# Attention softmax: row sums from ScalarE over query-major scores, one reciprocal and one transpose a unit

## The reference

```python
q = _rotary((_ln(x, qn_w, qn_b) @ q_w + q_b) ...); k = _rotary(...)      # per head
qn, kn = _ln(q, ln_w, ln_b), _ln(k, ln_w, ln_b)
scores = jnp.einsum('bhqd,bhkd->bhqk', qn, kn) / np.sqrt(HD)
attn = jax.nn.softmax(scores, axis=-1)
a = jnp.einsum('bhqk,bhkd->bhqd', attn, v)
x = layernorm(x + a @ out_w + out_b)
```

## Time and profile before

| | us |
|---|---|
| median of 3 runs | 2387.8 (2382.08 to 2388.36) |
| profiled execution | 2387.83 |
| its span | 2385.8 |
| attention phase within it, to the last row of its output sum | about 1277 |
| one pass of the loop (four units), 310.22 to 457.20 | 146.98 |
| busy PE, DVE, ACT, POOL over the span | 82%, 66%, 38%, 40% |

### The profile page before, as it was taken

The page is one execution under the profiler, slowest core; times in us unless marked ns, Lnnn a source line. Parts: engine busy times, 40 slices in busy tenths (PEclk is TensorE's granted clock), DMA queues, the critical chain, the costliest instruction groups (busy, mean ns, idle before and its releaser), DMA issues. The chain is left out here.

```text
span 2385.8 us, 30230 instructions
## 1 busy us (share of the span) xinstructions
PE 1949.7 (82%) x9560; PEld 1408.7 (59%) x9560; DVE 1564.9 (66%) x2942; ACT 913.2 (38%) x1532; POOL 955.1 (40%) x849
## 2 busy tenths in 40 slices
PE   4588887988889889899884999999948887878872
PEld 4455554655555556556533888887836665666651
DVE  4558578586785857757654666767544776777765
ACT  2134343443433444344342222222214555555653
POOL 1657657576565756657520222222101211221121
PEclk9689999999999999999887999999978998999885
DMA  4132132221322213222214121111031121022111
GB/s 130 27 89 54 28 106 48 84 53 44 88 53 79 53 50 81 53 62 54 67 49 149 50 83 58 53 53 53 18 110 36 53 71 54 18 70 71 54 36 53
DMA packets 90746, 148.67 MB, mean 62 GB/s; under 512 B 16560, under 2 KB 19632, under 8 KB 90672
## 3 DMA queue, kind: packets, MB, share of 16 engines
q1 hardware_dynamic: 90672, 147.76, 20.8%
HBM read 63.82 MB, written 33.55 MB: 41 GB/s over the span
## 5 line engine op out<-in xcount | busy, mean ns | idle before, releaser
L464 DVE TENSOR_REDUCE a_neg_max<-a_max 128x1 f32<-128x512 f32 x512 | 340.2, 686 | 255.4 <-PE a_max L720 250.3
L626 ACT ACTIVATE a_probs<-a_exp 128x512 f32<-128x512 f32 x512 | 291.0, 595 | 546.9 <-PE a_exp L735 542.5
L697 PE MATMUL a_t<-a_w_hi,a_zT_hi 128*128 128x384 f32 x512 | 200.1, 391 | 98.9 <-DVE a_v L430 87.7
L720 PE MATMUL a_max<-a_stack 96*128 96x512 f32 x512 | 228.4, 472 | 40.0 <-DVE a_neg_max L464 35.8
L311 POOL TENSOR_TENSOR a_rstd<-a_rstd,a_minus_half 128x16 f32<-128x16 f32 x64 | 186.3, 2912 | 131.1 <-DVE a_rstd L449 131.1
L1477 POOL TENSOR_TENSOR f_mixed<-f_tw,f_beta 128x512 f32<-128x512 f32 x64 | 96.1, 1521 | 352.2 <-DVE f_beta L1576 178.4
L735 PE MATMUL a_exp<-a_stack 100*128 100x512 f32 x512 | 196.9, 427 | 8.2 <-ACT a_stack L617 5.9
L698 PE MATMUL a_t<-a_w_lo,a_zT_hi 128*128 128x384 f32 x512 | 190.7, 373 | 0.0
L699 PE MATMUL a_t<-a_w_hi,a_zT_lo 128*128 128x384 f32 x512 | 190.2, 371 | 0.0
L720 PEld LDWEIGHTS a_max<-a_stack 96*128 96x128 f32 x512 | 104.0, 203 | 143.9 <-DVE a_neg_max L464 89.9
L697 PEld LDWEIGHTS a_t<-a_w_hi,a_zT_hi 128*128 128x128 f32 x512 | 111.3, 217 | 122.8 <-DVE a_v L430 103.8
(11 more groups left out here) (239 smaller groups left out, 4944.6 us busy)
## 6 DMA issues: line engine op xcount, KB each, us to landing
a_stack<-a_nT_hi SPq DMA_DIRECT2D x512, 64.0 KB, 2.0
a_stack<-a_nT_lo SPq DMA_DIRECT2D x256, 64.0 KB, 2.0
a_z<-x SPq DMA_DIRECT2D x8, 1024.0 KB, 6.9
a_y<-x SPq DMA_DIRECT2D x8, 1024.0 KB, 5.3
x<-a_y SPq DMA_DIRECT2D x8, 1024.0 KB, 4.2
r_xn<-x SPq DMA_DIRECT2D x8, 1024.0 KB, 5.7
r_cn<-ctx SPq DMA_DIRECT2D x8, 1024.0 KB, 7.8
x<-r_xn SPq DMA_DIRECT2D x8, 1024.0 KB, 4.3
```

The lines of the kernel that those rows point to most:

```text
L464: nc.vector.tensor_reduce(neg_max[:, t, ROW + h:ROW + h + 1], bank_max[i % 2][:, :], AX_X, ALU.max, negate=True).then_inc(max_done, 1)
L626: nc.scalar.activation(probs[:, kt % 2, h, :], bank_exp[i % 2][:, :], ACT.Exp, scale=float(1.0 / np.sqrt(np.float32(HD)))).then_inc(exp_do ...
L697: mm(bank, zT_hi[:, k, at], w_hi[:, k, g, :], start=k == 0, stop=False)
L720: mm(bank_max[i % 2][:, :], stack[0:ROW, par, h, t * P:(t + 1) * P], stack[0:ROW, par, HG + h, :], start=True, stop=True).then_inc(score_d ...
```

## The change

The scale 1/sqrt(32) moves from the exponential into the weights and biases of the query side's head norm, once, on POOL. The tile of ones, `bank_sum` and the 16 matmuls a unit with ones go; the freed bank becomes a third query-score bank. After `row_max` has found the maximum of a query-major tile, ACT takes the exponential of the same tile in place with that maximum as bias and with a sum along the row (`sum_exps`), and only that frees the bank. DVE then needs one reciprocal of 128x16 and one spreading copy a unit (`invert`), PE turns the result by four transposes (`spread_inverse`), ACT saves it (`save_inverse`), and one product of 128x512 normalises `bank_o` at the unit's last step. The tables move: `save_qkv` to steps 0, 1, 4, 7 and ahead of the other work of its step, the input's transposes to steps 12 and 13 and their saves to 13 and 14, the input statistics over two units. The diff, cut:

```diff
-DVE_STEPS, POOL_STEPS = 55, 40
+DVE_STEPS, POOL_STEPS = 31, 40
 KS_DONE = tuple(min(4 * (i + 1) // 3, T * HG) for i in range(16))
 QS_DONE = tuple(min(max(4 * (i - 1) // 3, 0), T * HG) for i in range(16))
-PROJECT_DONE = (4, 6, 8, 10, 12, 14, 15, 16, 16, 16, 16, 16, 16, 16, 16, 16)
+PROJECT_DONE = (4, 8, 9, 10, 12, 14, 15, 16, 16, 16, 16, 16, 16, 16, 16, 16)
 WEIGH_AT = (5, 7, 10, 13)
-TURN_AT, SAVE_AFTER = ((8, 11), (8, 10)), ((1, 2, 4, 7), (2, 3, 5, 8))
+TURN_AT, SAVE_AFTER = ((8, 11), (8, 10)), ((0, 1, 4, 7), (0, 1, 4, 7))
 OUT_AT, ADD_AFTER = (4, 5, 7, 9), (4, 6, 8, 10)
-Z_AT, Z_HIGH_AT, Z_LOW_AFTER = (12, 13, 14, 15), (13, 14, 15, 15), (13, 14, 15, 15)
+Z_AT, Z_HIGH_AT, Z_LOW_AFTER = (12, 12, 13, 13), (13, 13, 14, 14), (13, 13, 14, 14)
 MAX_AT, SAVE_MAX_AT = 14, 14
-X_NORM_AT, STATS_AFTER, FINAL_AFTER, SHIFT_AFTER = (6, 7, 8, 9), (6, 9, 11, 13), 6, 13
+X_NORM_AT, STATS_AFTER, FINAL_AFTER, SHIFT_AFTER = (6, 7, 8, 9), (5, 7), 9, 4
 MEAN_AFTER, VAR_AFTER, SQUARE_AT = (0, 1), (3, 4), (1, 2)
 TURN_HIGH_AT, TURN_LOW_AFTER = ((9, 12), (9, 11)), ((10, 13), (10, 12))
-NORM_AFTER, ATTN_HIGH_AT, ATTN_LOW_AFTER = (15, 15, 0, 1), 2, 3
+INVERT_AFTER, INVERSE_AT, INVERSE_SAVE_AT, ATTN_HIGH_AT, ATTN_LOW_AFTER = 1, 11, 12, 0, 0
+NB = 3
 SIDES = (1, 0)
 ROW = 3 * HD
...
-        bank_max = [ps("max0"), ps("max1")]
+        bank_max = [ps("max0"), ps("max1"), ps("max2")]
         bank_exp = [ps("exp0"), ps("exp1")]
-        bank_o, bank_sum = ps("o"), ps("sum")
+        bank_o = ps("o")
         bank_t = [ps("t0"), ps("t1")]
...
             pool.wait_ge(pool_step, steps.next())
+            for a in (head_w, head_b):
+                last = nc.gpsimd.tensor_scalar(a[:, :], a[:, :], float(1.0 / np.sqrt(np.float32(HD))), None, ALU.mult)
+            last.then_inc(pool_step, 1)
+            pool.wait_ge(pool_step, steps.next())
             for s in range(2):
                 rotate(0, s)
...
-                nc.vector.tensor_reduce(neg_max[:, t, ROW + h:ROW + h + 1], bank_max[i % 2][:, :], AX_X, ALU.max,
-                                        negate=True).then_inc(max_done, 1)
-            def normalise(W, c):
-                at = slice(c * P, (c + 1) * P)
-                if c == 0:
-                    dve.wait_ge(pv_done, T * W + T)
-                nc.vector.reciprocal(inverse[:, at], bank_sum[:, at]).then_inc(dve_step, 1)
+                        dve.wait_ge(summed, T * HG * U)
+                nc.vector.tensor_reduce(neg_max[:, t, ROW + h:ROW + h + 1].bitcast(F32R), bank_max[i % NB][:, :], AX_X,
+                                        ALU.max, negate=True).then_inc(max_done, 1)
+            def invert(U):
+                dve.wait_ge(summed, T * HG * (U + 1))
+                if counts(U):
+                    dve.wait_ge(inverse_done, U)
+                nc.vector.reciprocal(sums[:, :, :], sums[:, :, :]).then_inc(dve_step, 1)
                 dve.wait_ge(dve_step, steps.next())
-                last = nc.vector.tensor_tensor(bank_o[:, at], bank_o[:, at], inverse[:, at], ALU.mult)
-                if c < T - 1:
-                    last.then_inc(dve_step, 1)
-                    dve.wait_ge(dve_step, steps.next())
-                else:
-                    last.then_inc(attn_done, 1)
+                nc.vector.tensor_copy(inverses[:, :, :].rearrange("p t (h i) -> p t h i", h=HG),
+                                      sums[:, :, :].unsqueeze(3).broadcast_to((P, T, HG, HD))).then_inc(inverted, 1)
+            def normalise(W):
+                dve.wait_ge(pv_done, T * W + T)
+                dve.wait_ge(inverse_saved, W + 1)
+                nc.vector.tensor_tensor(bank_o[:, :], bank_o[:, :], inverse[:, :], ALU.mult).then_inc(attn_done, 1)
             def attn_low(W, g):
...
                             row_max(U + 1, m)
-                    for c in range(T):
-                        if i == NORM_AFTER[c] and i < 8 and counts(U):
-                            normalise(U - 1, c)
+                    if left >= 3 and i in SAVE_AFTER[g > 0]:
+                        t = SAVE_AFTER[g > 0].index(i)
+                        save_qkv(U + 3, (g + 3) % G, t, bank_t[0 if g == 0 else t % 2])
                     if i == ATTN_LOW_AFTER and counts(U):
                         attn_low(U - 1, (g - 1) % G)
...
                         if left >= 2 and i == TURN_LOW_AFTER[g > 0][s]:
                             turn_low(U + 2, s, bank_t[s])
-                    if g == 2 and more and i in STATS_AFTER:
-                        x_stats(b + 2, STATS_AFTER.index(i))
+                    if g >= 2 and more and i in STATS_AFTER:
+                        x_stats(b + 2, 2 * (g - 2) + STATS_AFTER.index(i))
                     if g == 3 and more and i == FINAL_AFTER:
                         x_final(b + 2)
-                    if g == 3 and more and i == SHIFT_AFTER:
-                        x_shift(b + 2)
+                    if g == 0 and left == 4 and counts(b) and i == SHIFT_AFTER:
+                        x_shift(b + 1)
                     for t in range(T):
                         if g == 0 and counts(b) and i == ADD_AFTER[t]:
                             add_out(b - 1, t, bank_t[1])
                         if g == 0 and left == 4 and i == Z_LOW_AFTER[t]:
                             z_low(b + 1, t)
-                    for c in range(T):
-                        if i == NORM_AFTER[c] and i >= 8:
-                            normalise(U, c)
+                    if i == INVERT_AFTER:
+                        invert(U)
+                    if i == T * HG - 1:
+                        normalise(U)
             for t in range(T):
                 x_stats(0, t)
...
+            def sum_exps(U, i):
+                h, t = divmod(i, T)
+                act.wait_ge(max_done, T * HG * U + i + 1)
+                if i == 0 and counts(U):
+                    act.wait_ge(inverted, U)
+                nc.scalar.activation(bank_max[i % NB][:, :], bank_max[i % NB][:, :], ACT.Exp,
+                                     bias=neg_max[:, t, ROW + h:ROW + h + 1],
+                                     accum_out=sums[:, t, h:h + 1]).then_inc(summed, 1)
+            def save_inverse(U):
+                act.wait_ge(inverse_done, U + 1)
+                if counts(U):
+                    act.wait_ge(attn_done, U)
+                nc.scalar.activation(inverse[:, :], bank_t[0][:, :], ACT.Copy).then_inc(inverse_saved, 1)
...
-                nc.scalar.activation(probs[:, kt % 2, h, :], bank_exp[i % 2][:, :], ACT.Exp,
-                                     scale=float(1.0 / np.sqrt(np.float32(HD)))).then_inc(exp_done, 1)
+                nc.scalar.activation(probs[:, kt % 2, h, :], bank_exp[i % 2][:, :], ACT.Exp).then_inc(exp_done, 1)
             def attn_hi(W, g):
                 act.wait_ge(attn_done, W + 1)
@@ -637,20 +658,25 @@
                 for i in range(T * HG):
                     for m in within(KS_DONE, i):
                         exps(U, m)
+                    if left >= 1 and i >= 1:
+                        for m in within(QS_DONE, i - 1):
+                            sum_exps(U + 1, m)
                     if i == ATTN_HIGH_AT and counts(U):
                         attn_hi(U - 1, (g - 1) % G)
+                    if i == INVERSE_SAVE_AT:
+                        save_inverse(U)
                     for s in range(2):
                         if left >= 2 and i == SQUARE_AT[s]:
                             square(U + 2, s)
                         if left >= 2 and i == TURN_HIGH_AT[g > 0][s]:
                             turn_high(U + 2, s, bank_t[s])
-                    if i == SAVE_MAX_AT and left >= 1:
-                        save_max(U + 1, (g + 1) % 2)
                     for t in range(T):
                         if g == 0 and left == 4 and i == X_NORM_AT[t]:
                             x_norm(b + 1, t)
                         if g == 0 and left == 4 and i == Z_HIGH_AT[t]:
                             z_high(b + 1, t)
...
                     pe.wait_ge(stacked[h], 6 * 16 * (U + 1))
+                if i == 0 and counts(U):
+                    pe.wait_ge(summed, T * HG * U)
                 if i == 1 and counts(U):
                     pe.wait_ge(maxrow_saved, U)
-                if i >= 2:
-                    pe.wait_ge(max_done, T * HG * U + i - 1)
-                mm(bank_max[i % 2][:, :], stack[0:ROW, par, h, t * P:(t + 1) * P], stack[0:ROW, par, HG + h, :],
+                if i >= NB:
+                    pe.wait_ge(summed, T * HG * U + i - NB + 1)
+                mm(bank_max[i % NB][:, :], stack[0:ROW, par, h, t * P:(t + 1) * P], stack[0:ROW, par, HG + h, :],
                    start=True, stop=True).then_inc(score_done, 1)
             def transpose_max(U):
                 pe.wait_ge(max_done, T * HG * (U + 1))
+                pe.wait_ge(summed, T * HG * U + T * HG - 2)
                 for t in range(T):
                     last = nc.tensor.transpose(bank_max[1][0:ROW + HG, t * P:(t + 1) * P], neg_max[:, t, :], ident[:, :])
```

(30 more changed lines are left out.)

29 lines of the change are left out of this document (15 added, 14 removed).

## The result

The changed kernel takes 2502.7 us (2500.0 to 2505.6) against 2387.9 us, a ratio of 1.0487 with a 95% interval of 1.0466 to 1.0508: 115 us slower. I had forecast 72 slower, 2460, with a range up to 2515. The profiled execution's span is 2498.2 us, 112.4 more than before.

A forecast was written before the change was run, and what follows sets the result against it. PE's pace plus a few stops bounds the attention phase. Seven passes at +6.4 (+45), first unit and last sequence (+5) and the clock (+22) add 72 us to 2388: 2460, range 2395 to 2515.

The forecast's parts named there:

- The ring: PE, key score, exponential, row-sum exponential, next step's query score: passed once a step whatever the banks, 2.18 us a turn.
- S: ACT's new exponential of query-major scores (sum_exps), with its sum forecast to end 0.85 us after its start, bounds 0.70 and 0.95.
- E: ACT's exponential of key-major scores; forecast 0.44 us behind its key score, and 0.49 to the next activation.
- The rival of the third bank: Query-score banks: the third hides the sums, so PE runs on its work; 2200 us, chance of a result under 2381: 0.13.
- Removed work and g = 0: PE nets 3.3 us less work a unit; with early saves and transposes g = 0 takes 46.1 us against 51.6.
- the two gains: In g = 0: early saves start item 4 4.6 us sooner; early input transposes start the next unit 4.4 sooner.
- the 4.4 a pass of the early transposes: End of g = 0: next unit starts about 1.6 us behind the maxima's transposition instead of 6.0.
- the low stretch at t = 7 to 13: Units g = 1 to 3, us from first projection item: PE little busy, low clock afterwards; +1.0 a unit, +22 over 22 units.
- The rival of the low clock: Later steps of the units: the clock stays low there too, 3.5 us a unit instead of 1.0; 2520 us, chance 0.11.
- Its units lose some 3 us each: Last sequence, without projections: loss by the same ring; with the very last unit and the first unit's sums, +5 us together.
- the 16 S in a row: First unit: its 16 row-sum exponentials stand in a row, priced within +5 us together with the last sequence.
- The draw: Whole kernel: the same ring at about 1.9 us a turn leaves the time at 2388 us; chance 0.07.

The follow-up runs named there:

- e1: Changed kernel with ACT's sum_exps of step i - 1 moved ahead of exps of step i, nothing else; 2270.4 us, 0.9508 of the kernel before.
- e3: Changed kernel with sum_exps as a plain exponential, without accumulating row sums (sums a constant 1); 2474.6 us.
- e10: e8 with ACT's order set back to the change's: exps of step i ahead of sum_exps of step i - 1; 2498.6 us.
- e5: Changed kernel without sum_exps altogether (sums a constant 1), query scores waiting for the row maximum instead; 2217.0 us, 0.9296 of the kernel before.
- e8: e1 with three moves: DVE's invert first, second save of turned heads a step later, second square behind the first sum; 2223.6 us, 0.9312 of the kernel before.
- b1: Kernel before with the change's tables of the input's transposes and save_max behind their copies; 2370.2 us, 0.9926.
- b2: b1 with the change's early saves of the projections and projection items at 4, 8, 9 too; 2341.6 us, 0.9812 of the kernel before.
- e6: Changed kernel with 22 idle, never-read products ahead of query scores 9, 10, 12, 13 and 15 of units g = 1 to 3; 2481.1 us.
- e4: Changed kernel with nine idle, never-read products ahead of query scores 13 and 15 of units g = 1 to 3; 2484.5 us.

## Why the prediction was right, and where it was off

**The ring: right, in place and size.** Between the first release and the last waiting score of g = 3 I had nine steps that sum to 23.9 us; they take 23.3. S ends 0.77 after its start, not 0.85 (the read of the accumulator adds 0.11, not 0.15), and from a key score to its E it is 0.43 to 0.49, where I had 0.44. S's own row is 0.66 to 0.68, not 0.695; whether that is because it writes in place in PSUM or because it is another function than the row I took it from, no run tells. The waits add up to 9.1 us in that unit, where I had some 10. e1, e3 and e10 show the cause.

**The rival of the third bank: right price, wrong condition for this order.** 2200 was its time; e5 takes 2217 and e8 2224, the latter with three moves that the rival didn't have, and e1, without them, 2270. The rule of the Trainium skill's "Perfetto Trace Analysis", section "Matmuls", to rotate independent groups through different banks, is borne out only in e1's order, which e8 has too; with three banks in the change's order the overlap doesn't come, as the prediction had it.

**Removed work and g = 0: right in sum.** g = 0 takes 46.9 us against 46.1, its save waits are 0.58 and 0.25 us. But b1 and b2 show the two gains at 18 and 29 us on the kernel before where the terms had 31 and 32: the 4.4 a pass of the early transposes is half given back ahead of the maxima. Why the sum held in the changed kernel all the same no run isolates. Its g = 0 has its own waits for sums, at which the transposes may stand for nothing; that is a guess.

**Where the sum was off: the clock, and what stands at the two ends of a unit.** I put the low stretch at t = 7 to 13 and took +1.0 a unit. It comes at steps 12 to 15 and the next unit's first items, where nothing hides it. In g = 3 the way to the first sum takes 11.0 us, forecast 9.9, since the first key score stands behind four items, the first two and most of the third at 1.2 GHz, and goes 3.4 us after the start of the unit (406.71 against 403.29) where I had 2.3. The prediction let the square gate the first sum at t = 6.6, because DVE's head mean stands behind fewer operations. It didn't see that `attn_low`, now ahead of that mean, waits for `attn_hi`, which stands behind the first key score's E. So the delay passes through E, `attn_hi`, `attn_low`, the mean and POOL's centring to the square, which comes at 7.7:

```profile
408.32 0.69 DVE L493 TENSOR_TENSOR a_attnT_lo<-a_o,a_attnT_hi 128x512 fp32r<-128x512 f32 x1 [0.69 <-ACT a_attnT_hi L654]
410.98 0.63 ACT L611 ACTIVATE a_turn<-a_n 128x512 f32<-128x512 f32 x1 [0.92 <-POOL a_n L308]
```

In e6's unit at the full clock this way is 10.3 us, so 0.7 of the 1.1 is the clock; there the first key score, 2.6 after the start, waits for the maxima's spread. From the last waiting score to the next unit it takes 3.3, forecast 2.2, since `weigh`, which I had inside the waits, comes after the last of them and paces PE. Together +2.3, less 0.6 of the shorter turns: 37.63 instead of 36.0. Over a pass this is 4.1 us more than the 9.4 forecast (6.4 and three times 1.0), 21 us in the five middle passes. The rival of the low clock had another place, since the turns of this unit run at full clock, and a size (3.5 a unit) above the 2.3 that e6's trace gives.

**The other place: the first and the last sequence.** "Its units lose some 3 us each" was a difference to units of 33 us. At the end of the attention phase, without the input's work, four units outside g = 0 take 30.5, 30.5, 29.0 and 26.1 us in the kernel before, from spread to spread. The ring hardly gets shorter when work drops out, and in the changed kernel they take 38.9, 39.7, 38.6 and 33.5. The clock has a part in it that no run separates: in the last two of them it is 0.61 and 0.65, in the kernel before 0.82 and 0.80. And the sum had no ring in unit 0, which takes 49.4 instead of 41.4 us, while the 16 S in a row that it did price cost nothing (-0.3 ahead). Together the outer parts make +44.6 (-0.3, 22.4, 38.4, -7.2 and -8.7) where the sum had 25: the other 20 of the 40 us that the span grew beyond the forecast. The -8.7 is luck: it lies in phases that the change doesn't touch, and without it the forecast would have missed by 49.

**The range and the rivals' sums.** Its upper end came from a longer S and a clock cost of 2 us a unit. S was shorter, and the rest came from the ends of the units and from the outer parts, which had no bounds; that 2503 lies within 2515 is partly luck. Two sums of rivals don't come out. The draw asks for 0.15 a turn beyond a free accumulator read and no loss of clock, but these two give 60 of the 72 us, so 0.05 would have done. The rival of the low clock leaves 0.35 us a unit for items beside nine turns of 0.35, while one item alone costs 0.44 more at 1.2 GHz (0.96 instead of 0.52).

## What to carry to other kernels

When work moves to an engine with room, ask in which order its queue takes it, not how much it is: a wait that is released behind work which itself depends on the waiting engine's next instruction is a ring, and the step can't be shorter than it. Look for it by following one release backwards until you meet your own engine; if you do, swap the two in the queue before you add buffers, and check that the buffers suffice for the new order. A ring's floor hardly falls when other work drops out, so compare it to the shortest unit too, and put the price of a low clock where PE's idle time ends, not where it is.

## What the runs showed of the hardware that I had not expected

- An accumulating exponential of 128 x 512 in place in PSUM takes 0.66 to 0.67 us in most rows (mean 677 ns), its `ACTIVATION_READ_ACCUMULATOR` starts 0.57 after its start and ends 0.77 after it; without the accumulation the waiting score goes 0.11 us sooner. Two of them behind each other start 0.66 apart (434.92 and 435.58 in the changed kernel), where in e3 two without the sum take 1.24 together, so some 0.58 apart.
- The phases that the change doesn't touch took 1093.4 us before and 1084.7 after, with the same 3960 products. In the profiled executions of seven kernels with the changed attention phase, the changed kernel among them, they took 1084.1 to 1084.9, in four others 1090.1 to 1090.5, and in b1 and b2 1094.7 and 1094.2. The granted clock is 0.91 in both rows above and PE busy 888 against 883 us, so I take it for low stretches that fall on other places of the same work; that is a guess, and no run isolates it. A forecast for this kernel is uncertain by some 10 us for this alone.
- Idle products that fill one wait move the low clock to the next thin stretch (e4) and can themselves wait (e6, 0.37 us): as a remedy they gave 18 and 22 us, the move of one loop 232.
